# Delta-rule attention and expert layer: the instruction order of the attention stage, and its routing steps, rewritten

## The reference

```
x = x + attention(layernorm(x))
x = x + experts(layernorm(x))

attention: q, k (4 heads of 128), v, g (4 heads of 64), beta = sigmoid(x Wb)
           k = k / |k| ; q = q * 128^-0.5
           for each token t:  pred = k_t S ; S = S + k_t (beta_t (v_t - pred)) ; o_t = q_t S
           o = o * rsqrt(mean(o*o) + 1e-5) * norm_w * g * sigmoid(g) ; return o Wo

experts:   probs = softmax(x router^T) ; the two largest of 8 per token, with their probabilities
           out = sum over the two experts of prob * gelu(x w1^T) w2^T    (hidden width 1024)
```

## Time and profile before

| | us |
|---|---|
| median of 3 runs | 1017.46 |
| profiled execution | 1013.14 |
| its span, first to last instruction | 1011.3 |
| TensorE busy | 870.1 |
| VectorE busy | 638.9 |
| ScalarE busy | 612.0 |
| GpSimd busy | 422.9 |

### The profile page before, as it was taken

The page is one execution under the profiler, slowest core; times in us unless marked ns, Lnnn a source line. Parts: engine busy times, 40 slices in busy tenths (PEclk is TensorE's granted clock), DMA queues, the critical chain, the costliest instruction groups (busy, mean ns, idle before and its releaser), DMA issues. The chain is left out here.

```text
span 1011.3 us, 29922 instructions
## 1 busy us (share of the span) xinstructions
PE 870.1 (86%) x9998; PEld 682.0 (67%) x9999; DVE 638.9 (63%) x1822; ACT 612.0 (61%) x1636; POOL 422.9 (42%) x426
## 2 busy tenths in 40 slices
PE   0689998989888899888985099999999999999884
PEld 0468876777767777777874077777777777767662
DVE  3468897788877888878883545555555555543442
ACT  4579887778877787876763255445445445543330
POOL 2345545566665656555433503323323323221213
PEclk9999999999999999999986589999999999999997
DMA  5212222222222322211111613233233233322212
GB/s 189 62 49 85 78 67 80 70 91 86 86 90 69 96 70 91 76 64 60 41 35 39 211 33 58 44 48 56 43 47 54 45 47 53 49 45 42 32 24 27
DMA packets 49736, 66.58 MB, mean 66 GB/s; under 512 B 6416, under 2 KB 34192, under 8 KB 49616
## 3 DMA queue, kind: packets, MB, share of 16 engines
q1 hardware_dynamic: 35616, 46.33, 15.5%
q0 software_dynamic: 13424, 18.10, 10.3%
q10 hardware_dynamic: 576, 0.53, 0.2%
HBM read 41.46 MB, written 23.48 MB: 64 GB/s over the span
## 5 line engine op out<-in xcount | busy, mean ns | idle before, releaser
L933 PE MATMUL ps<-w_s,wqk 128*128 128x128 f16 (+1 forms) x1336 | 244.3, 292 | 11.6 <-ACT wqk L662 8.9
L645 POOL DMA_INDIRECT out<-wvg_s,yidx x71 | 113.5, 1598 | 317.7 <-DVE wvg_s L1818 159.2
L933 PE MATMUL ps<-x_s,w_hi 128*128 128x256 f16 (+1 forms) x1376 | 201.4, 256 | 0.1
L662 ACT ACTIVATE w_s<-ps 128x512 f16<-128x512 f32 (+2 forms) x288 | 144.5, 523 | 47.5 <-PE ps L933 39.4
L933 PE MATMUL ps<-x_s,w_lo 128*128 128x256 f16 (+1 forms) x688 | 170.1, 255 | 0.0
L933 PEld LDWEIGHTS ps<-w_s,wqk 128*128 128x128 f16 x1336 | 107.2, 102 | 85.7 <-issue 16.0
L1791 DVE SCALAR_TENSOR_TENSOR KpAT<-KQ,wqk 128x512 f16<-128x512 f32 (+1 forms) x144 | 98.7, 685 | 100.8 <-ACT wqk L662 100.7
L933 PE MATMUL ps<-w_s,KpAT 128*128 x568 | 155.5, 274 | 0.0
L933 PEld LDWEIGHTS ps<-x_s,w_hi 128*128 x1376 | 120.5, 98 | 17.8 <-issue 0.6
L662 ACT ACTIVATE x_s<-ps 128x512 f16<-128x512 f32 x36 | 21.5, 597 | 163.5 <-PE ps L1308 163.5
L909 ACT ACTIVATE KQ<-ps 128x512 f32<-128x512 f32 (+1 forms) x144 | 85.1, 591 | 48.4 <-PE ps L933 42.9
(11 more groups left out here) (187 smaller groups left out, 1841.7 us busy)
## 6 DMA issues: line engine op xcount, KB each, us to landing
wst<-w SPq DMA_DIRECT2D x56, 256.0 KB, 2.7
w_s<-eye SPq DMA_DIRECT2D x32, 256.0 KB, 2.7
rowA<-routed_rows SPq DMA_DIRECT2D x28, 260.0 KB, 2.8
x_s<-x SPq DMA_DIRECT2D x32, 128.0 KB, 2.6
out<-x_s SPq DMA_DIRECT2D x32, 128.0 KB, 1.7
rowA<-routed_rows SPq DMA_DIRECT2D x15, 130.0 KB, 2.1
KQ<-w SPq DMA_DIRECT2D x6, 256.0 KB, 3.8
out<-wvg_s,yidx POOLq DMA_INDIRECT x71, 3.9
```

Source lines behind the costliest of these rows:

```text
L645: pool.indirect_dma_start(out=out, out_offset=bass.IndirectOffsetOnAxis(ap=yidx[:, q, a:a + 1], axis=0), in_=yrow[:, q % 2, a, :], in_offs ...
L662: return act.activation(dst, src, ACT.Copy, scale=scale)
L933: return pe.matmul(dst, lhsT, rhs, start=start, stop=stop, **kw)
```

## The change

Four things are written differently.

1. The order of the calls in a turn of the loops of TensorE, ScalarE, GpSimd and VectorE, and with it which tile a call of the turn is for. SyncE's loop starts at another point of the same cycle.
2. The scatter of a tile is parted: its first DMA (`k = 0`) in one turn, the second in the next.
3. The routing generator is gone. Each step is a function of its own with its own place in the turn; a group is spread over four turns. A step waits for the step that it needs (`follows()`), not for every counted step.
4. Most routing steps, `k_norm`'s first and `o_scale` become SCALAR_TENSOR_TENSOR, some with a constant tile as second input; two constants are added to `fc`.

`rank` and the exponentials of a group are taken at its last tile rather than counted from its first, and `gram` waits for positions in its second half alone.

```diff
             for i in range(T + POOL_SKEW):
-                kscale_(i - 2)
                 ln2_scale(i - 5)
-                l_low(i - 3)
                 split_lo(2 * (i) + 0)
-                scatter(i - 11)
+                scatter(i - 12, 1)
                 ln1_scale(i)
                 o_rsqrt(i - 4)
                 split_lo(2 * (i) + 1)
+                kscale_(i - 1)
+                scatter(i - 11, 0)
+                l_low(i - 2)
...
-                reach(pe, s_pos, Ranked.n)
+                if a == 1:
+                    reach(pe, s_pos, Ranked.n)
...
             for i in range(T + ACT_SKEW):
+                scale_piece(2 * (i - 1) + 0)
+                r_half(i - 4)
+                xnT_evac(i - 2)
...
+                xn2T_evac(i - 6)
+                ln1(i - 1)
+                split_hi(2 * (i - 1) + 1)
...
-                ln1(i)
-                xn2T_evac(i - 5)
-                split_hi(2 * (i) + 1)
...
-                link(dve.tensor_scalar(karg[:, H:2 * H], eb[:, :], 1.0, A_SCALE ** 2, ALU.add, ALU.mult))
+                link(dve.scalar_tensor_tensor(karg[:, H:2 * H], eb[:, :], 1.0, k_square_scale.broadcast_to([P, H]), ALU.add, ALU.mult))
...
+            def follows():
+                dve.wait_ge(s_dve, Chain.at)
+
+            def link_of_chain(ins):
+                step(ins)
+                Chain.at = Own.base + Own.n
...
-                step(dve.tensor_tensor(first, a0[:, :, :], col(tm[:, :], E), ALU.is_equal))
-                step(dve.tensor_scalar(rows[:, :, D + 2], tm[:, :], -1.0, float(E), ALU.mult, ALU.add))
-                yield
...
+            def first_expert(n):
+                g = routed_group(n)
+                if g is None:
+                    return
+                follows()
+                step(stt(rows_of(g)[:, :, D + 2], tm[:, :], -1.0, pref[:, 0:1].broadcast_to([P, C]), ALU.mult, ALU.add))
+                link_of_chain(stt(first, a0[:, :, :], 1.0, col(tm[:, :], E), ALU.mult, ALU.is_equal))
...
+            def first_gate(n):
+                g = routed_group(n)
+                if g is None:
+                    return
+                follows()
+                step(stt(rows_of(g)[:, :, D + 3], fc[:, 529 + C * g:529 + C * (g + 1)], 1.0, ones[:, 0:C], ALU.mult, ALU.mult))
+                link_of_chain(stt(rows_of(g)[:, :, D + 1], g1[:, :], 1.0, rows_of(g)[:, :, D], ALU.mult, ALU.subtract))
...
-                    Route.gen = route(n // C)
...
+                residual(i - 5)
+                y_masked(i - 4, 4)
+                positions(i - 9)
+                kT_low(i - 3)
+                chosen_positions(i - 9)
+                best_marked(i - 7)
...
-SP_SKEW = 7
-POOL_SKEW = 11
-ACT_SKEW = 9
-PE_SKEW = 9
-DVE_SKEW = 11
-RANK_AFTER = 7
+SP_SKEW = 6
+POOL_SKEW = 12
+ACT_SKEW = 7
+PE_SKEW = 7
+DVE_SKEW = 10
+RANK_AFTER = 5
```

More of the change, by code:

```diff
@@ L478, in _ @@
                 piece(2 * (i - 2) + 1)
+                piece(2 * (i - 1) + 0)
+                store(i - 6)
             for k in range(LATE):
@@ L609, in scatter @@
                 pool.wait_ge(s_slot, g + 1)
[L610 to L613, removed]
+                pool.indirect_dma_start(
+                    out=routed, out_offset=bass.IndirectOffsetOnAxis(ap=slot[:, g % 2, k, c:c + 1], axis=0),
+                    in_=rowA[:, g % RG * C + c, :], in_offset=None).then_inc(s_scat[g % RG][c], 16)
             pool.memset(rowA[:, C:2 * C, :], 0.0).then_inc(s_spare, 1)
@@ new lines, in _, with stt @@
+            class Chain:
+                at = 0
+            def follows():
[3 more added lines that the diff above has]
+                Chain.at = Own.base + Own.n
+            def stt(out, in0, scalar, in1, op0, op1):
+                return dve.scalar_tensor_tensor(out, in0, scalar, in1, op0, op1)
+            diff, ex, a0, a1, a3 = r8
+            m1, tm, m2, ssum, g2, g1 = r1
+            pref_c = pref.unsqueeze(1).broadcast_to([P, C, E])
@@ new lines, in without_first, with next_logit, next_marked @@
+            def without_first(n):
+                if routed_group(n) is None:
+                    return
+                follows()
+                link_of_chain(stt(a1[:, :, :], first, -1e30, diff[:, :, :], ALU.mult, ALU.add))
+            def next_logit(n):
+                if routed_group(n) is None:
+                    return
+                follows()
+                link_of_chain(dve.tensor_reduce(m2[:, :], a1[:, :, :], AX.X, ALU.max))
+            def next_marked(n):
+                if routed_group(n) is None:
+                    return
+                follows()
+                link_of_chain(stt(a0[:, :, :], a1[:, :, :], 1.0, col(m2[:, :], E), ALU.mult, ALU.is_equal))
@@ new lines, in next_ranked, with next_rank, second_expert @@
+            def next_ranked(n):
+                if routed_group(n) is None:
+                    return
+                follows()
+                link_of_chain(stt(a3[:, :, :], a0[:, :, :], 1.0, pref_c, ALU.mult, ALU.mult))
+            def next_rank(n):
+                if routed_group(n) is None:
+                    return
+                follows()
+                link_of_chain(dve.tensor_reduce(tm[:, :], a3[:, :, :], AX.X, ALU.max))
+            def second_expert(n):
+                if routed_group(n) is None:
+                    return
+                follows()
+                link_of_chain(stt(second, a3[:, :, :], 1.0, col(tm[:, :], E), ALU.mult, ALU.is_equal))
@@ L1613, in route_masks, with expert_masks, exp_sum @@
+            def expert_masks(n):
+                if routed_group(n) is None:
+                    return
+                follows()
+                stt(both[:, :, :], first, 1.0, second, ALU.mult, ALU.add).then_inc(s_both, 1)
+            def exp_sum(n):
+                g = routed_group(n)
+                if g is None:
+                    return
                 dve.wait_ge(s_rexp, g + 1)
                 step(dve.tensor_reduce(ssum[:, :], ex[:, :, :], AX.X, ALU.add))
-                step(dve.tensor_tensor(a0[:, :, :], ex[:, :, :], second, ALU.mult))
@@ L1704, in _ @@
-                residual(i - 6)
-                kT_low(i - 4)
-                routing()
-                y_masked(i - 5, 4)
-                v_gate(i - 4)
-                routing()
-                xnT_low(i - 3)
-                masked_l(i - 4)
+                without_first(i - 8)
                 masked_scores(i - 4)
-                routing()
+                next_logit(i - 8)
                 level_zero_t(i - 4)
+                slots(i - 10)
+                y_masked(i - 5, 5)
+                o_scale(i - 6)
```

276 lines of the change are left out of this document (140 added, 136 removed).

## The result

The changed kernel takes 974.05 us, the median of 4 runs (971.99 to 980.22), where the kernel before took 1016.02 (4 runs, 1013.85 to 1020.03). The ratio is 0.9606, 95% interval 0.9569 to 0.9642: about 4% faster. Forecast were 978 us and a range of 964 to 1002.

What follows compares the result with a forecast made beforehand. Routing-related waits were taken to stretch 24 attention tiles to 15.84 us against 14.03 undisturbed. At 14.2 a tile, 39.4 us go: 1013.1 - 39.4 = 973.7, plus 4.3 gives a 978 us median, range 964 to 1002.

Steps and rivals of the forecast that it cites:

- the 4.3 that were added for it: Whole execution: the profiled run is 4.3 us under the median, added to turn 973.7 into 978.
- (a): TensorE: with rank ahead of first_w, gram's 11.6 us of waits for positions go; kT_low late by at most 2.4 us.
- (b): GpSimd and ScalarE: parting the scatters and taking xn2T ahead of ln1 removes most of 13.3 us of logits waits.
- (c): VectorE: routing in 19 places removes three slow steps, 2.3 us per group, 14 us of VectorE over 6 groups.
- (d): TensorE's tile loop: x_make(4) moves between kT and gram, the sum stays 14.03 us; bounded by ±0.3 a tile, taken as none.
- The 0.17 above the sum: Attention tile: 0.17 us over 14.03, for routing on an 87% full VectorE and the staging-buffer loop, giving 14.2.
- (e): GpSimd's loop through the weights' staging buffer: 13.90 us with a scatter, 12.40 before; costed at nothing, +0.5 for the range.
- The fifth rival: Staging-buffer loop becomes the bound: 16.4 us a tile, 13 us slower, 1031 us; chance 0.06.
- (f): Start and drain: nearly the same order; drain -1 to +2 us, taken as 0; edges -2 to +2 in the range.
- The second: VectorE too full, routing between steps TensorE waits for: 14.94 us a tile, gain 21.7, 996 us; chance 0.22.
- The third: New VectorE form waits beside GpSimd's subtractions as before: 14.8 us a tile, gain 25, 992 us; chance 0.13.
- The fourth: No change, waits move to the next queue: 15.7 to 15.95 us a tile, 1017 us; chance 0.04.

Runs made afterwards that it cites:

- run 3: Changed kernel with rank directly ahead of gram again, both gram halves waiting for positions; 986.74 us, ratio 0.9681 to the kernel before.
- run 10: Changed kernel with a tile's two scatters paired ahead of ln1's scale, a turn later, and ln1 ahead of xn2T; 986.93 us, ratio 0.9722 to the kernel before.
- run 7: Kernel before with one swap, xn2T ahead of ln1 on ScalarE; 1016.61 us, ratio 0.9960.
- run 11: Changed kernel with routing steps in ten places, a group in two turns, positions behind v_gate, rank a turn earlier; 988.92 us, ratio 0.9741 to the kernel before.
- run 12: Changed kernel with ScalarE's ln1 moved to just ahead of first_w's evacuation; 975.59 us, ratio 0.9618 to the kernel before.
- run 2: Kernel before with the SCALAR_TENSOR_TENSOR forms alone, every instruction in its old place; 1019.30 us, ratio 0.9995.
- run 1: Changed kernel with the old instruction forms (tensor_tensor, tensor_scalar, copy) in the new places; 980.28 us, ratio 0.9607 to the kernel before.
- run 4: Changed kernel with a tile's two scatters paired ahead of ln1's scale, xn2T still ahead of ln1; 1018.86 us, ratio 0.9987 to the kernel before.
- run 9: Changed kernel with the two scatters paired ahead of ln1's scale, a turn later so the slots are ready; 980.54 us, ratio 0.9666 to the kernel before.
- run 8: Changed kernel unaltered, on the second chip; 982.66 us, ratio 0.9631 to the kernel before.

## Why the prediction was right

The waits that were named are gone, and the period is 14.26 against 14.2. The 24 tiles gained 38.0 us where 39.4 was forecast. That the profile's whole gain is 39.9 is partly luck: the edges added 1.9, of which 1.7 is a first gram that begins early in this one profile. The profiled execution, 973.25 us, was forecast at 973.7; the median, 974.05, lies 4 us under the forecast since the 4.3 that were added for it aren't there this time. By its steps:

**(a) Rank ahead of first_w.** Right: no wait on `run`, and run 3 brings one stall per group back. In the new order the old place costs about 6.5 us, less than the 11.6 of the wait, since the stall that comes back is shorter (6.8 us in all).

**(b) The pair parted, xn2T ahead of ln1.** Right as a mechanism: waits on ScalarE are 1.9 us in place of 13.3. "Most of 13.3" is the wait; as time, the two undone in the changed kernel cost 1.1% (run 10), 11 us, and the swap done alone in the kernel before returned at most 4 us (run 7). The two halves cover each other in part, which the prediction took together and so didn't count twice.

**(c) Routing in 19 places** (the loop has 20). The slow steps did go: TENSOR_SCALAR of 1.00, and the two of 0.93 and 0.87 us, are 0.19, 0.18 and 0.16. VectorE's busy time in the stretch fell by 312.0 - 302.1 = 9.9 us, where 14 was forecast. The saving of (0.93 + 1.00 + 0.87) - (0.19 + 0.18 + 0.16) = 2.3 us per group, 6 groups, held: summed line by line, VectorE's instructions of the stretch take 343.9 us in place of 357.9. Busy time counts instructions that overlap once, and so fell by less. What the prediction doesn't say is how two of the three lay on the path. In the kernel before they stand right ahead of x_make(4)'s mask and of nL:

```profile
202.01 0.94 DVE L1597 TENSOR_TENSOR chosen<-r,r 128x32 f32<-128x32 f32 x1
202.21 1.47 PE L933 MATMUL ps<-KQ 128*128 128x256 f16 x12
202.85 1.16 POOL L587 TENSOR_TENSOR w_lo<-wst,w_hi 128x512 f16<-128x512 f32 x1
202.87 1.17 DVE L1598 TENSOR_SCALAR rowA<-r 128x4 f32<-128x4 f32 x1
205.38 0.68 DVE L1470 TENSOR_TENSOR nL<-ps,fc 128x512 f32<-128x512 f32 x1
206.15 0.63 ACT L662 ACTIVATE Lh<-nL 128x512 f16<-128x512 f32 x1 [0.69 <-DVE nL L1470]
```

Lh starts 3.94 us behind gram here, against 2.39 in an undisturbed tile. Five tiles are like this (3.88 to 3.94). In the sixth, at 457.88, the first step takes 0.94 us but the second only 0.16, and Lh starts 2.92 behind gram. That is some 8 us of the 38. The prediction ties the slow steps to the 8.2 us of waits on masked levels and doesn't name the delay of nL; its sum starts from an undisturbed tile and so holds them all the same. Routing dense, with positions late and rank earlier, costs 1.3% (run 11).

**(d) The rest of TensorE's order.** The forecast sum of 8.24 + 3.67 + 2.12 = 14.03 came out as 8.07 + 3.67 + 2.34 = 14.08. The first part gave up 0.17 and the last took 0.22, which is x_make(4) changing sides, as argued. The ±0.3 was right to be taken as none. What the argument missed is that ScalarE's queue from Lh to eb would be just as long as TensorE's first part, with no slack. The 0.17 above the sum came out as 0.18 (14.26 over 14.08): five tiles where ScalarE waits for the weights (2.0 us) and two where nL is late (0.8) are most of it.

**(e) The staging loop.** Costed at nothing, and there: 2.1 us of waits in the stretch, and the longest tile of the profile, 14.85 us from 350.73, has one of them:

```profile
356.09 0.63 ACT L663 ACTIVATE w_hi<-wst 128x512 f16<-128x512 f32 x1 [0.75 <-DMA wst<-w]
```

Run 12, with 13.4 us of such waits, shows that it stands just under the bound, as the sums 13.90 and 14.03 had it. split_lo ended 1.2 us behind the gram (222.89 + 1.16 against 222.87), forecast was 1.7. The fifth rival, slower, would have needed 3.6.

**(f) Edges.** Start -1.7, first seven tiles +1.1, drain -1.4, experts +0.1: -1.9 together, within the -2 to +2, with a start in it that other runs didn't have.

**The rivals.** The second (VectorE too full, 996) failed: 88% full (302.1 of 342.2), and only 3.8 us of waits on masked levels. The third (the new form waits as the old one did, 992) was right about the chip and wrong about the place: its rule is run 2, its price of 2.3 us per group wasn't paid because the new places don't stand beside a subtraction. When one does, the step waits here too. That happens three times in the changed kernel between 100 and 500 us (0.53, 1.23 and 0.48 us), against the sign "no small VectorE instruction over 0.3 us". The longest:

```profile
165.66 1.16 POOL L588 TENSOR_TENSOR w_lo<-wst,w_hi 128x512 f16<-128x512 f32 x1
165.68 1.23 DVE L1595 SCALAR_TENSOR_TENSOR at<-chosen,pos 128x64 f32<-128x64 f32 x1
```

The step starts 0.02 us behind the subtraction and ends 0.09 us behind it, at 1.23 us where the other five take 0.23. The exposure of the former copy, which the prediction feared, is there too where the place is bad: in run 11 that step (`rowA<-fc`) stands beside l_low in all six groups and takes 0.54 to 0.71 us, against 0.16 in the changed kernel. The fourth (waits move on, 1017) is what run 7 looks like for a part done alone, not the whole.

**How the parts add.** Undone one at a time in the changed kernel, by ratio to run 1 on the same chip: rank's place 0.7%, pair and order 1.1%, spread with late positions 1.3% (1.0% and 1.2% for the last two against run 12 of their own session). The last holds a part of the first. Together they are at most 3.1 of the 3.9%; the remainder, the rest of TensorE's and VectorE's order and how the parts help each other, isn't shown by a run. No run did the spread of routing alone in the kernel before.

The two profiles show where in the tile it lies. Summed over the 24 tiles, gram to Lh fell from 66.7 to 58.3 us, mostly the two slow routing steps. Lh to eb fell from 169.3 to 149.1: ScalarE's ln1 waited 14.6 us for its scale before and doesn't now, and x_make(4) left, some 4 us. Eb to kT fell from 79.8 to 78.6. KT to the next gram fell from 64.4 to 56.2: six stalls of 2.3 us on rank and its positions went, 13.7, and x_make(4) came in at 0.22 a tile. That is 8.4 + 20.2 + 1.3 + 8.2 = 38.

## What to carry to other kernels

When a small two-input VectorE step takes 1 us for 0.2 us of work, look at what GpSimd does beside it, and move the step; another form of the same step changes nothing. How much it gains depends on what the step delays: 1.5 us in one tile of four here, where nL stood behind it. A step whose result another engine waits for at one place of a cyclic order (rank and its positions, scatter and its slots) wants other work between producer and consumer, and one turn of slack in place of none decides: the pair of scatters in a turn where the slots aren't ready took back the whole gain (run 4, 38.6 us over run 1), and one turn later the pair alone costs 0.6% (run 9). And write down every loop that closes over a tile with its sum before easing one: here three stood within some 0.2 us of each other (TensorE's order, ScalarE's queue, the staging buffer), and easing one by 0.62 us gave nothing.

## What the runs showed of the hardware

- A VectorE step of 128x4 to 128x64 with two SBUF inputs that starts inside GpSimd's 128x512 subtraction (1.16 us) ends when that ends, in either form: SCALAR_TENSOR_TENSOR of 128x4 takes 0.89 and 1.17 us there (run 2), and 0.15 to 0.19 elsewhere. So does the TENSOR_SCALAR of 128x4 with one SBUF input: 1.17 us in five times of the kernel before, 0.16 in the sixth.
- It waits for the end rather than going slower: one such step of 128x64 took 1.23 us beside a subtraction of 1.16, against 0.23 in its five other times, and it ended 0.09 us behind the subtraction.
- Not every step waits. Beside the same subtractions a two-input step with one input in PSUM (`pos<-ps,run`) took 0.18 us in six of six times in run 8, reductions to 128x4 0.15 to 0.19, and a TENSOR_SCALAR of 128x1 0.15.
- Not every GpSimd instruction holds a step up. The 128x8 power (`kscale`, 1.64 us) has two SBUF inputs as well, and the SCALAR_TENSOR_TENSOR of 128x32 with two SBUF inputs that starts inside it in the kernel before took 0.18 us in six of six times.
- Issuing one indirect DMA held GpSimd for 1.04 to 1.11 us in the 44 times of the changed kernel's stretch, with some 0.18 us of idle time before it (7.6 us in 43 times).
- The granted clock of the stretch rose from 0.98 to 1.00 of 2.4 GHz when TensorE's idle share fell from 11% (41.7 of 380.2) to 4.5% (15.5 of 342.2).
